# Attention walked by pairs of units, with transposes, scores and value products of a group in two parts

## The reference, cut to what matters

```python
q = (xn @ Wq) ; k, v = xn @ Wkv                  # one k and v for all heads, and a null key in front
sim = einsum('bhid,bjd->bhij', q, k) + bias      # layer 1 and 3: bias by relative position; layer 2: an input
sim = where(causal | masked, -big, sim)
attn = softmax(sim, axis=-1)
out = einsum('bhij,bjd->bhid', attn, v)          # then out @ Wout, a layer norm, and x + that
```

## Time and profile before

| | us |
|---|---|
| median of three runs | 2386.2 |
| the profiled execution | 2377.6 |
| its span, first to last instruction | 2375.8 |
| busy in that span: PE / PE weight loads | 2012.2 / 1425.0 |
| busy: DVE / ACT / POOL | 1693.6 / 1350.9 / 1091.4 |

### The profile page before, as it was taken

How to read it: one execution, slowest core, us unless ns; L and a number is a source line. 1 busy time by engine, 2 the same in 40 slices (tenths; PEclk the granted TensorE clock), 3 DMA queues, 4 the chain that set the end, 5 groups by cost and what they waited for, 6 DMA issues and landing times. The chain is left out here.

```text
span 2375.8 us, 46869 instructions
## 1 busy us (share of the span) xinstructions
PE 2012.2 (85%) x11738; PEld 1425.0 (60%) x11738; DVE 1693.6 (71%) x4082; ACT 1350.9 (57%) x2900; POOL 1091.4 (46%) x1286
## 2 busy tenths in 40 slices
PE   5996495999999989388889999985586999999978
PEld 4885463666666657366556666664454666666657
DVE  5777665888888866557668888745566788888845
ACT  2222564766777654137557777633465777777743
POOL 1442112666766642006556666611123666766622
PEclk8998697999999999699999999987796999999989
DMA  3530356333343323187777778731455433343332
GB/s 112 161 126 17 100 173 236 98 107 107 113 125 116 108 69 111 48 308 219 213 229 231 231 231 236 232 133 37 139 183 181 121 106 106 109 121 109 106 110 86
DMA packets 222215, 338.76 MB, mean 143 GB/s; under 512 B 27446, under 2 KB 104380, under 8 KB 222044
## 3 DMA queue, kind: packets, MB, share of 16 engines
q1 hardware_dynamic: 222044, 336.86, 45.2%
HBM read 250.63 MB, written 102.91 MB: 149 GB/s over the span
## 5 line engine op out<-in xcount | busy, mean ns | idle before, releaser
L1481 POOL TENSOR_SCALAR at_row<-at_row,at_inv 128x129 f32<-128x129 f32 (+7 forms) x384 | 745.2, 1941 | 386.8 <-DVE at_inv L1639 382.7
L1686 ACT ACTIVATE at_row<-at_row,at_nmax 128x129 f32<-128x129 f32 (+7 forms) x768 | 595.7, 776 | 238.5 <-DVE at_nmax L1658 232.6
L1658 DVE CUSTOM_DVE_ANT_0 at_row<-at_s,bias,at_row 128x128 f32<-128x128 f32 (+7 forms) x768 | 623.2, 811 | 79.0 <-PE at_s L1586 51.5
L1598 PE MATMUL at_t<-ident,at_row 128*128 128x128 f32 x3456 | 541.5, 284 | 86.4 <-DVE at_row L1481 58.9
L1598 PEld LDWEIGHTS at_t<-ident,at_row 128*128 128x128 f32 x3456 | 391.1, 143 | 286.4 <-issue 103.5
L1585 PE MATMUL at_s<-k_hh,q_hl 128*128 128x512 f32 (+3 forms) x1152 | 464.0, 403 | 34.7 <-SPq L1547 25.9
L1614 PE MATMUL at_o<-at_pt,v 128*64 128x512 f32 (+3 forms) x2304 | 438.9, 503 | 7.9 <-ACT at_pt L1679 3.8
L1586 PE MATMUL at_s<-k_lp,q_h 65*128 65x512 f32 (+3 forms) x1152 | 393.1, 353 | 0.0
L1679 ACT ACTIVATE at_pt<-at_t 128x512 f32<-128x512 f32 (+2 forms) x576 | 308.8, 537 | 140.0 <-PE at_t L1598 133.8
L1496 DVE COPY at_pt<-at_t 128x128 f32<-128x128 f32 (+3 forms) x576 | 278.6, 484 | 149.8 <-PE at_t L1598 149.3
L1481 DVE TENSOR_SCALAR at_row<-at_row,at_inv 128x129 f32<-128x129 f32 (+7 forms) x384 | 253.3, 660 | 37.4 <-DVE at_inv L1639 24.6
(11 more groups left out here) (225 smaller groups left out, 2907.6 us busy)
## 6 DMA issues: line engine op xcount, KB each, us to landing
q_hl<-q_dram SPq DMA_DIRECT2D x192, 256.0 KB, 4.4
bias<-bands_dram SPq DMA_DIRECT2D x64, 512.0 KB, 5.6
q_dram<-pj_qh SPq DMA_DIRECT2D x96, 256.0 KB, 2.7
q_dram<-pj_ql SPq DMA_DIRECT2D x96, 256.0 KB, 2.8
q_h<-q_dram SPq DMA_DIRECT2D x96, 256.0 KB, 5.1
o_dram<-at_o_sb SPq DMA_DIRECT2D x96, 256.0 KB, 4.6
o_in<-o_dram SPq DMA_DIRECT2D x10, 2048.0 KB, 8.5
bands_dram<-brow_dram SPq DMA_DIRECT2D x2, 8192.0 KB, 31.6
```

Of the source, the lines that this page charges most:

```text
L1481: return eng.tensor_scalar(cells, cells, inv[:, i:i + 1], None, ALU.mult)
L1598: last = eng.transpose(t_ps[m % NTR][:, c * P:(c + 1) * P], row[:, u % RING, here:here + P], t["ident"][:])
L1658: eng.tensor_tensor_reduce(out=row[:, u % RING, ZERO:ZERO + width], in0=s_ps[u % 2][:, 0:width], in1=bt[:, lo:lo + width], scale=-1.0, sca ...
L1686: eng.activation(cells, cells, ACT.Exp, scale=-1.0, bias=nmax[:, i:i + 1], accum_out=rsum[:, i:i + 1]).then_inc(s["exp"], 1)
```

## The change

The step now counts pairs of units. PE's step n transposes unit 2n - 4, computes the scores of 2n + 4, transposes 2n - 3, computes the scores of 2n + 5, and in every second step adds a half of a group's value products: the first half two steps behind the group's last transposes, the second half two steps later. The other engines' steps are written in pairs too. Groups, tiles, buffers, operands and the number of instructions of each kind are as they were.

```diff
-    VALUES_AT = (0, 2, 4)
+    PARTS, GAP = 2, 2
+    LAG = 2
     ZERO = 4
-    EARLY, LATE = 5, 11
+    EARLY, LATE = 3, GU // 2 + LAG
+    PAIRS = U // 2
...
+    def values_of(n):
+        g, at = divmod(n - LAG - GU // 2, GU // 2)
+        return g, at // GAP if at % GAP == 0 else None
...                                        # PE, values
-                    n = len(VALUES_AT)
-                    cut = [k * blocks // n * 2 for k in range(n + 1)]
-                    for j, side in products[cut[part]:cut[part + 1]]:
+                    n = len(products) // PARTS
+                    for j, side in products[part * n:(part + 1) * n]:
...                                        # PE, step
-                    u = n - 2
-                    if has(u, U):
-                        transposes(turn, u)
-                    if has(n + 3, U):
-                        logits(turn, n + 3)
-                    g = u // GU - 1
-                    if u % GU in VALUES_AT and has(g, NGRP):
-                        values(turn, g, VALUES_AT.index(u % GU))
+                    for side in range(2):
+                        if has(n - LAG, PAIRS):
+                            transposes(turn, 2 * (n - LAG) + side)
+                        if has(n + 2, PAIRS):
+                            logits(turn, 2 * (n + 2) + side)
+                    g, part = values_of(n)
+                    if part is not None and has(g, NGRP):
+                        values(turn, g, part)
...                                        # DVE, step
-                    if n % 2 == 1 and has(n, U):
-                        inverse(turn, n - 1)
-                    if has(n - 3, U):
-                        evacuate(eng, turn, n - 3, eng.tensor_copy, 1, "ev_d")
-                    if n % 2 == 1 and has(n, U):
-                        normalize_even(turn, n - 1)
-                    if has(n + 2, U):
-                        add_bias(turn, n + 2)
+                    if has(n + 1, PAIRS):
+                        add_bias(turn, 2 * (n + 1))
+                    if has(n, PAIRS):
+                        inverse(turn, 2 * n)
+                    if has(n - LAG, PAIRS):
+                        evacuate(eng, turn, 2 * (n - LAG), eng.tensor_copy, 1, "ev_d")
+                    if has(n + 1, PAIRS):
+                        add_bias(turn, 2 * (n + 1) + 1)
+                    if has(n, PAIRS):
+                        normalize_even(turn, 2 * n)
+                    if has(n - LAG, PAIRS):
+                        evacuate(eng, turn, 2 * (n - LAG) + 1, eng.tensor_copy, 1, "ev_d")
...                                        # ACT, step
-                    if has(n - 3, U):
-                        evacuate(eng, turn, n - 3, copy, 0, "ev_a")
-                    if has(n + 1, U):
-                        exponent(turn, n + 1)
-                    g = (n - 7) // GU - 1
-                    if (n - 7) % GU == 0 and has(g, NGRP):
+                    for side in range(2):
+                        if has(n - LAG, PAIRS):
+                            evacuate(eng, turn, 2 * (n - LAG) + side, copy, 0, "ev_a")
+                        if has(n + 1, PAIRS):
+                            exponent(turn, 2 * (n + 1) + side)
+                    g, part = values_of(n)
+                    if part == PARTS - 1 and has(g, NGRP):
                         output(turn, g)
...                                        # POOL, step
-                    if n % 2 == 0:
-                        return
-                    if has(n - 1, U):
-                        normalize_odd(turn, n)
-                        null_weights(turn, n - 1)
-                    if has(n + 5, U):
-                        null_logits(turn, n + 5)
+                    if has(n, PAIRS):
+                        normalize_odd(turn, 2 * n + 1)
+                        null_weights(turn, 2 * n)
+                    if has(n + 3, PAIRS):
+                        null_logits(turn, 2 * (n + 3))
```

More of the change, by code:

```diff
@@ L1615, in values @@
                                           pt[g % 2][:, side, at + i0:at + BANK], start=j == 0, stop=j == blocks - 1)
-                    if part == n - 1:
+                    if part == PARTS - 1:
                         last.then_inc(s["pv"], 1)
                 def step(turn, n, has):
-                    u = n - 2
-                    if has(u, U):
-                        transposes(turn, u)
-                    if has(n + 3, U):
-                        logits(turn, n + 3)
-                    g = u // GU - 1
-                    if u % GU in VALUES_AT and has(g, NGRP):
-                        values(turn, g, VALUES_AT.index(u % GU))
+                    for side in range(2):
[6 more added lines that the diff above has]
+                        values(turn, g, part)
                 start(eng, s, marks, "qk", "tr", "pv")
-                run_halves(eng, step, place, TURNS, U, EARLY, LATE)
+                run_halves(eng, step, place, TURNS, PAIRS, EARLY, LATE)
             @block.vector
@@ L1700, in step @@
                 def step(turn, n, has):
-                    if has(n - 3, U):
-                        evacuate(eng, turn, n - 3, copy, 0, "ev_a")
-                    if has(n + 1, U):
-                        exponent(turn, n + 1)
-                    g = (n - 7) // GU - 1
-                    if (n - 7) % GU == 0 and has(g, NGRP):
+                    for side in range(2):
[5 more added lines that the diff above has]
+                    if part == PARTS - 1 and has(g, NGRP):
                         output(turn, g)
-                    if turn.known() and 0 <= turn.turn < TURNS and turn.half < B - 1 and n % 6 == 0 and 12 <= n < 36:
-                        out_weights(n // 6 - 2)
+                    if turn.known() and 0 <= turn.turn < TURNS and turn.half < B - 1 and n % 3 == 0 and 6 <= n < 18:
+                        out_weights(n // 3 - 2)
                 start(eng, s, marks, "exp", "ev_a", "out")
-                run_halves(eng, step, place, TURNS, U, EARLY, LATE)
+                run_halves(eng, step, place, TURNS, PAIRS, EARLY, LATE)
                 eng.wait_ge(s["out"], NGRP * (B * TURNS + 1))
@@ L1744, in step @@
                 def step(turn, n, has):
-                    if turn.known() and 0 <= turn.turn < TURNS and turn.half < B - 1 and n % 6 == 2 and 14 <= n < 38:
-                        low_weights(n // 6 - 2)
-                    if n % 2 == 0:
-                        return
-                    if has(n - 1, U):
-                        normalize_odd(turn, n)
-                        null_weights(turn, n - 1)
-                    if has(n + 5, U):
-                        null_logits(turn, n + 5)
+                    if turn.known() and 0 <= turn.turn < TURNS and turn.half < B - 1 and n % 3 == 1 and 7 <= n < 19:
+                        low_weights(n // 3 - 2)
+                    if has(n, PAIRS):
[3 more added lines that the diff above has]
+                        null_logits(turn, 2 * (n + 3))
                 start(eng, s, marks, "norm_p", "null_in", "null_out")
-                run_halves(eng, step, place, TURNS, U, EARLY, LATE)
+                run_halves(eng, step, place, TURNS, PAIRS, EARLY, LATE)
 def close_layer(nc, t, out):
```

## The result

The changed kernel takes 2473.9 us (2470.76 to 2478.42, 4 runs) against 2384.4 us for the kernel before on the same chip: ratio 1.0381, 95% interval [1.0355, 1.0407], 3.8% slower. Forecast were 2426 us with 2365 to 2470. The sign was right, the size was not: of about 90 us, 50 were missing. The profiled execution (2478.42 us) has a span of 2476.6 us. The two profiled executions lie 100.8 us apart, the medians 89.5: the profiled one of before (2377.6 us) is quicker than its other runs, that of after the slowest of its four.

The account below looks back on a forecast made before the run. PE (51.6 us of work in a 56.7 us turn) and DVE were both taken as near their limit, order deciding who waits. 2377.6 + 40 = 2418 us, as a median of runs 2426 us; range 2365 to 2470 us.

Parts of the forecast that it names:

- The sign: Whole kernel: slower, with a chance of 0.75, against 0.18 for faster and 0.07 for the same.
- the main term: Attention turns: longer value-product pieces make DVE wait 16.7 us instead of 12.4, so 58.9 us a turn, 2.2 more.
- DVE's wait behind the eight products: Behind tile 3's second addition, DVE waits 3.35 us for eight 512-wide value products and the transposes behind them.
- near 360: Evacuations on DVE: their waits for PE sum to near 24 x 15 = 360 us, against 149.3 us before.
- The port: DVE scaling beside GpSimd: DVE comes second but is let in after about 0.8 us, gaining 2.1 us a turn.
- the 2540 us: Rival, chance 0.05: GpSimd keeps the shared port to its end, DVE's scalings wait, 5 us a turn, +115 us.
- Its sum: Attention: 21 turns x 2.2 = +46 us, less 6 us for first turns, +40 us over three layers.
- first turns 2 us shorter: Each layer's first turn: no earlier turn's products, so two large waits are missing; 2 us shorter, -6 us in all.
- Three layers: +40 us: All three attention layers: +46 us from 21 turns and -6 us from first turns, counted alike.
- layer 2's two jumps: Two layer-2 turns where the loop jumps back, about 20 us standing together: no change, bounds -20 and +15 us.
- lock step: Attention turns: PE cannot run ahead of DVE before the value products, and DVE cannot pass them; no separate size.

Follow-up runs that it names:

- whole: best_c with the value products whole again, eight blocks in two pieces, each behind a step's scores: 2401.7 us, ratio 1.0101 to the kernel before.
- best_c: Changed kernel with halved product pieces between transposes and scores, evacuation behind both additions, layer-2 rows in new places, layer 1's jump between steps 10 and 11: 2359.2 us.
- between: Changed kernel with each part of the value products halved, a half between the transposes and scores of each unit of the pair: 2399.3 us, ratio 1.0085.
- jump: Changed kernel with the loop's jump between steps 10 and 11 (LATE 11 instead of 6), output weights' loads moved along: 2463.3 us, ratio 1.0353.
- rows_ring: Changed kernel with layer-2 rows of bias laid out to load 7 to 16 units ahead instead of 2 to 16: 2445.6 us, ratio 1.0270.

## Why the prediction was right and wrong

- *The mechanism of the main term held.* 58.9 us a turn were forecast; layer 3 shows 59.5. DVE's wait behind the eight products shown above was 2.85 us (3.35 forecast), evacuations wait 396.2 us in sum ("near 360"), 1025 columns are scaled in 0.86 us. That the pieces cause it is shown by whole against best_c, which differ in nothing else, and by between.
- *The port held.* Scalings by shape after the earlier trace rows, and POOL and DVE beside each other in layer 3:

```profile
L1487 DVE TENSOR_SCALAR at_row<-at_row,at_inv 128x1025 f32<-128x1025 f32 x48 | 41.2, 857 | 0.0
L1487 DVE TENSOR_SCALAR at_row<-at_row,at_inv 128x897 f32<-128x897 f32 x48 | 34.8, 724 | 1.4 <-issue 1.4
```

```profile
2200.75 3.25 POOL L1487 TENSOR_SCALAR at_row<-at_row,at_inv 128x1025 f32<-128x1025 f32 x1
...
2202.31 0.75 DVE L1487 TENSOR_SCALAR at_row<-at_row,at_inv 128x1025 f32<-128x1025 f32 x1
```

  DVE starts 1.56 us after POOL, takes its 0.75 us and ends 0.94 us before it. Of DVE's 48 scalings of 1025 columns, 31 started 1.26 to 1.75 us behind one of POOL's and took 0.75 us; nine started 0.05 to 0.83 us behind, took 1.61 to 0.83 us, and every one of them ended 1.66 us behind POOL's start, while POOL went on for another 1.2 us. Scaling fell from 253.3 to 208.5 us, 1.9 us a turn (2.1 forecast). The Trainium skill (SBUF — State Buffer, on the two separate sides) has the port pair locked for the whole instruction of who came first; this trace does not agree, and the 2540 us that hung on it did not come.
- *Its sum was a third too small.* I took first turns 2 us shorter; in layer 3 the first is 0.8 us longer, and the others are 2.8 us longer, not 2.2. That is 20.1 us in layer 3, 60 in three layers, where the sum had 40. The share of layers 1 and 2 is layer 3's carried over; adding the jump's 1.8 us in four turns of before to jump's +14.6 us in layer 1 gives 22, near it.
- *The step that failed* is "Three layers: +40 us", one turn walked and counted for all three layers alike, with nothing beside it but layer 2's two jumps "at no change, with bounds of -20 and +15 us". That last term was about right: these two turns are 9.7 us longer, 4 more than two other turns. What the sum put at nothing, without a reason, were layer 1's jumps and layer 2's loads.
- *Layer 1's jumps.* DVE now stands in lock step with PE, so its stand stops both, and the clock falls behind it: four turns take 4.5 instead of 1.8 us more than others, 11 us of the 12.1 that are left there beside the main term.
- *Layer 2's queries.* Of its 50.5 us 30.4 are left beside the main term; rows_ring gave 34.1 back, 9.7 of them in the two turns with the jump. I had written that SP's loads are "gated by the scores and the bias additions that are done" and left as they are; so they were. But PE now asks for the queries sooner. Before, at the start of one of the later turns of layer 2 (SP and PE):

```profile
1368.14 0.86 SPq L1410 DMA_DIRECT2D bias<-corners_dram  x2
...
1377.16 0.60 SPq L1396 DMA_DIRECT2D q_h<-q_dram  x1
...
1383.17 0.48 PE L1585 MATMUL at_s<-k_hh,q_hl 128*128 128x512 f32 x1
```

  SP began the turn's rows at 1368.14, and the scores that need these queries came 15.0 us later without a wait. In the stretch of after shown above SP began at 1361.16, and PE was ready for the same scores at 1373.51 (1376.39 less the wait of 2.88), only 12.35 us later and 2 us behind the issue of `q_h`, which landed at 1376.35. In all seven later turns PE is ready 12.3 to 12.6 us behind the addition that lets SP begin, where before it took 15.2 to 15.9, and the queries landed 13.9 to 15.6 us behind it in both. What this wait costs hangs on the pieces too: with the halves of between, and the same loads, most of it is gone.

By layers: 60 + 12 + 30 = 102 us, the three differences of the table, on the scale of the profiled executions; the medians differ by 89.5.

## What to carry to other kernels

Where a change makes one engine run further ahead, follow each buffer that it reads back to the queue that fills it and ask when that queue may begin: moving one load up in a full queue only hands the wait to the next. When two engines go in lock step, a stall that one of them used to absorb (here a jump, or a late load) becomes a stall of both, and TensorE's clock may fall behind it. Work that is put between a producer and its consumer should be cut as short as the slack there.

## What the runs showed of the hardware

- In after PE stood 1.8 to 3.4 us eleven times, at layer 1's four jumps and for the queries in layer 2's seven later turns; with ten of these stands the granted clock fell to half for 3 to 7 us, and sixteen records of 512 columns took 5.47 us instead of 3.65. Behind the layer's start, layer 1 had no such stretch before; after, it has four.
- At a loop's jump DVE stood between nothing and 9.5 us in after and jump, with one to three packets on the instruction queue during such stands; the longest of any run is 11.4 us, in layer 2 of between. Those of layer 1 in after are 2.6 to 2.9 us. That a fetch is the cause, and that other transfers lengthen it, is not shown.
